# Query and key low parts moved from GpSimd to VectorE, high parts stored by ScalarE, fewer and differently shaped transfers for the score stacks, and longer rings for two loads

## What is computed

```
x = layernorm(x + attn(x))        # 16 heads of 32: softmax(q k^T / sqrt(32)) v,
                                  # blended with a "splat" attention, out projection
x = layernorm(x + ssm(ctx, x))    # u = silu(conv(in_proj ctx)); state = state*exp(delta*A) + delta*u*B_t
                                  # y_t = sum_n state*C_t  over 16 states n, 512 steps; y*silu(x)
x = layernorm(x + ffn(x))         # ternary weights: silu(gate)*up, rms norm, down projection
```

## Time and profile before

| | before |
|---|---|
| median of 3 runs | 1502.52 us |
| the three runs | 1502.21, 1502.52, 1505.94 us |
| profiled execution | 1506.96 us, of which span 1504.9 us |
| mean granted TensorE clock | 0.861 |

### The profile page before, as it was taken

How to read it: one execution, slowest core, us unless ns; L and a number is a source line. 1 busy time by engine, 2 the same in 40 slices (tenths; PEclk the granted TensorE clock), 3 DMA queues, 4 the chain that set the end, 5 groups by cost and what they waited for, 6 DMA issues and landing times.

```text
span 1504.9 us, 14270 instructions
## 1 busy us (share of the span) xinstructions
PE 1215.9 (81%) x4693; PEld 566.1 (38%) x4698; DVE 1208.4 (80%) x1425; ACT 764.5 (51%) x1118; POOL 208.5 (14%) x243
## 2 busy tenths in 40 slices
PE   5563848777779997887989998888899978887996
PEld 4332313332244542332445533333355423333453
DVE  5877988888879998778789996888889996887323
ACT  6765433445367653635466742545476544452231
POOL 1000122001111123100111132100111231001001
PEclk7765877777969998979989998899799989888898
DMA  6853687455328968554239968444169695641131
GB/s 192 275 175 126 145 211 183 98 126 111 85 86 204 256 158 221 140 127 98 52 96 248 232 170 225 99 91 105 51 168 265 163 215 147 143 115 30 63 98 56
DMA packets 113688, 220.18 MB, mean 146 GB/s; under 512 B 15584, under 2 KB 26336, under 8 KB 113616
## 3 DMA queue, kind: packets, MB, share of 16 engines
q1 hardware_dynamic: 94240, 151.25, 33.5%
q0 software_dynamic: 18432, 67.12, 23.1%
q10 hardware_dynamic: 944, 0.92, 0.2%
HBM read 122.37 MB, written 29.62 MB: 101 GB/s over the span
## 4 chain that ended last, share of the span: by engine, by line
PE 35%; DVE 35%; issue 8%; ACT 5%; DMA 5%; POOL 1%; SPq 1%; DVEq 0%; ACTq 0%; POOLq 0%
DVE ST L867 13%; PE ps L1460 8%; DVE ST L859 5%; PE ps L1269 5%; DVE MX L923 5%; PE ps L1252 5%; PE ps L1420 4%; PE ps L1404 3%; DMA WP<-proj_tiles 3%; DVE ST L870 2%; PE ps L1361 2%; PE ps L1333 2%; PE ps L1220 1%; DVE BST L903 1%; ACT dA L568 1%
## 5 line engine op out<-in xcount | busy, mean ns | idle before, releaser
L867 DVE TENSOR_TENSOR_SCAN ST<-dA,ST 128x1024 f32<-128x1024 f32 x128 | 312.5, 2441 | 8.8 <-ACT dA L568 6.0
L1460 PE MATMUL ps<-V,GU 128*128 128x512 f16 x1024 | 239.1, 389 | 5.9 <-DVE V L1054 5.6
L473 POOL DMA_DIRECT2D YA<-ST x128 | 109.7, 857 | 960.2 <-DVE ST L870 911.5
L923 DVE TENSOR_REDUCE MX<-ps 128x1 f32<-128x512 f32 x256 | 165.2, 686 | 90.4 <-PE ps L1252 89.9
L568 ACT ACTIVATE dA<-DL,Aneg 128x511 f32<-128x511 f32 x256 | 168.3, 713 | 79.4 <-DVE ST L867 79.1
L700 ACT ACTIVATE PT<-ps 128x1024 f32<-128x1024 f32 x128 | 126.3, 1020 | 124.8 <-PE ps L1361 124.0
L1252 PE MATMUL ps<-KS,QS 96*128 96x512 f32 x256 | 127.3, 564 | 71.3 <-DVE MX L923 41.6
L870 DVE TENSOR_TENSOR ST<-ST,BC 128x1024 f32<-128x1024 f32 x128 | 159.4, 1246 | 4.4
L859 DVE TENSOR_TENSOR ST<-DU,BC 128x1024 f32<-128x1024 f32 x128 | 155.9, 1218 | 7.1 <-DMA BC<-bc_rows 7.1
L1420 PE MATMUL ps<-WP,QS 128*128 128x512 f32 x512 | 144.6, 426 | 9.3 <-DMA WP<-proj_tiles 8.8
L1460 PEld LDWEIGHTS ps<-V,GU 128*128 128x128 bf16 x1024 | 97.2, 100 | 143.1 <-issue 32.6
(11 more groups left out here) (229 smaller groups left out, 1600.2 us busy)
## 6 DMA issues: line engine op xcount, KB each, us to landing
YA<-ST POOLq DMA_DIRECT2D x128, 512.0 KB, 7.1
BC<-bc_rows SPq DMA_DIRECT2D x64, 512.0 KB, 6.2
qk_parts<-PT SPq DMA_DIRECT2D x64, 256.0 KB, 4.4
GU<-gu_tiles SPq DMA_DIRECT2D x64, 256.0 KB, 7.5
WP<-proj_tiles SPq DMA_DIRECT2D x64, 256.0 KB, 7.1
QS<-qk_parts SPq DMA_DIRECT2D x96, 128.0 KB, 3.4
KS<-qk_parts SPq DMA_DIRECT2D x96, 128.0 KB, 3.8
ST<-in_L_ffn_w_gate_up_dram SPq DMA_DIRECT2D x16, 256.0 KB, 3.3
```

The lines of the kernel that those rows point to most:

```text
L867: nc.vector.tensor_tensor_scan(flat, dA[:, a, :, :].rearrange("p e s -> p (e s)"), flat, 0.0, ALU.mult, ALU.add).then_inc(s_scan, 1)
L923: nc.vector.tensor_reduce(MX[:, j % 2, qt, h:h + 1], ps[:, n % 2, :], AX_X, ALU.max).then_inc(s_mx, 1)
L1460: last = mm(ps[:, f % F_RING, :], GU[:, t % GU_RING, k, m * P:(m + 1) * P], XHL[:, z, k, :], start=(k == 0 and z == 0), stop=(k == KT - 1 ...
```

## The change

1. The low parts leave POOL and are done by DVE, in the order of DVE's program: units 0 to 3 behind the halves at r = 5, 6, 7, 8 (`LOW_BEHIND`), unit 4 behind the half at r = 12, units 5, 6 and 7 behind max tiles 0-3, 4-9 and 10-15.
2. High parts are stored by ACT, right behind the cast, from its own DMA queue; SP keeps the low parts.
3. `qk_parts` in HBM is laid out as (batch, z, head, part, 32, 512) in place of (batch, z, part, 512, 512). A store of one part of a unit is now 4 heads x 32 x 512 with a gap between heads; in exchange the two parts that stand next to each other in a stack come in one load of 64x2x512, so a stack takes 8 loads in place of 12.
4. BC gets three slots in place of two: the load of state n waits for the products of n-3.
5. WP gets four slots and lies in QS[0], whose own tile is free after group 2; its loads stand two tiles further ahead in SP's program.

```diff
-        qk_parts = dram("qk_parts", (B, 2, 2, H, S))
+        qk_parts = dram("qk_parts", (B, 2, NH, 2, D, S))
...
-        BC = sb("BC", [P, 2, 2, S])
+        BC = sb("BC", [P, BC_RING, 2, S])
...
-        WP = sb("WP", [P, 2, H], F32R)
+        WP = QS[0]
...
+        LOW_BEHIND = (5, 6, 7, 8)
...
             def load_bc(bb, n):
-                if type(bb) is not int or bb > 0 or n >= 2:
-                    sp.wait_ge(s_prod, half(bb, n - 2, 1) + 1)
+                if n >= BC_RING:
+                    sp.wait_ge(s_prod, half(bb, n - BC_RING, 1) + 1)
+                else:
+                    since(sp, s_prod, half(bb, 0, 0))
...
-                    first_row = P * j + 2 * D * pair
-                    for r, (zq, zk) in enumerate(((0, 0), (0, 1), (1, 0))):
-                        for z, dst, part in ((0, QS[i], zq), (1, KS[i], zk)):
-                            src = qk_parts[b, z, part, first_row:first_row + 2 * D, :].rearrange("(h p) s -> p h s", p=D)
-                            sp.dma_start(dst[D * r:D * r + D, 2 * pair:2 * pair + 2, :].bitcast(F32), src).then_inc(s_stack[i][pair], 16)
+                    heads = slice(2 * pair, 2 * pair + 2)
+                    for z, dst in ((0, QS[i]), (1, KS[i])):
+                        parts = qk_parts[b, z, HG * j + 2 * pair:HG * j + 2 * pair + 2].rearrange("h a p s -> (a p) h s")
+                        both, high = (slice(D, 3 * D), slice(0, D)) if z == 0 else (slice(0, 2 * D), slice(2 * D, 3 * D))
+                        sp.dma_start(dst[both, heads, :].bitcast(F32), parts).then_inc(s_stack[i][pair], 16)
+                        sp.dma_start(dst[high, heads, :].bitcast(F32), parts[0:D]).then_inc(s_stack[i][pair], 16)
...
                 for u, (j, z) in enumerate(UNITS):
-                    sp.wait_ge(s_hi, 2 * NG * b + u + 1)
-                    sp.dma_start(qk_parts[b, z, 0, P * j:P * j + P, :], QKP[:, u % 2, :].bitcast(F32)).then_inc(s_part[u % 2], 16)
                     sp.wait_ge(s_lo, 2 * NG * b + u + 1)
-                    sp.dma_start(qk_parts[b, z, 1, P * j:P * j + P, :], QKP[:, 2 + u % 2, :].bitcast(F32)).then_inc(s_part[u % 2], 16)
+                    sp.dma_start(qk_parts[b, z, HG * j:HG * j + HG, 1], QKP[:, 2 + u % 2, :].bitcast(F32)).then_inc(s_part[u % 2], 16)
...
+                def load_wp(t):
+                    if t >= WP_RING:
+                        sp.wait_ge(s_dn, NT * b + t - WP_RING + 1)
+                    sp.dma_start(WP[:, t % WP_RING, :].bitcast(F32), proj_tiles[t]).then_inc(s_wp[t % WP_RING], 16)
+
...
                 for t in range(NT):
-                    if t >= 2:
-                        sp.wait_ge(s_dn, NT * b + t - 1)
-                    sp.dma_start(WP[:, t % 2, :].bitcast(F32), proj_tiles[t]).then_inc(s_wp[t % 2], 16)
+                    if t + WP_RING // 2 < NT:
+                        load_wp(t + WP_RING // 2)
...
                     nc.scalar.copy(QKP[:, u % 2, :], bank).then_inc(s_hi, 1)
+                    j, z = UNITS[u]
+                    act.wait_ge(s_hi, 2 * NG * b + u + 1)
+                    act.dma_start(qk_parts[b, z, HG * j:HG * j + HG, 0], QKP[:, u % 2, :].bitcast(F32)).then_inc(s_part[u % 2], 16)
                     for n, a in fill_halves(2 * KT + u, first):
                         exp_dA(b, n, a)
...
-                for r in range(2 * KT):
+                def low_part(u):
+                    dve.wait_ge(s_hi, 2 * NG * b + u + 1)
+                    if u >= 2:
+                        dve.wait_ge(s_part[u % 2], 32 * KT * b + 32 * (u // 2))
+                    nc.vector.tensor_tensor(QKP[:, 2 + u % 2, :], PT[:, 0, u % 2, :], QKP[:, u % 2, :].bitcast(F32),
+                                            ALU.subtract).then_inc(s_lo, 1)
+
+                for r in range(3 * KT):
                     fill_half(r)
-                for u in range(2 * NG):
-                    if u >= NG:
-                        max_tiles(b, 0, X_FIRST[u - NG], X_FIRST[u - NG + 1])
+                    if r in LOW_BEHIND:
+                        low_part(LOW_BEHIND.index(r))
+                for u in range(NG, 2 * NG):
+                    max_tiles(b, 0, X_FIRST[u - NG], X_FIRST[u - NG + 1])
                     fill_half(2 * KT + u)
+                    low_part(u)
```

More of the change, by code:

```diff
@@ L44 @@
 GU_RING = 3
+WP_RING = 4
+BC_RING = 3
 RING = 3
@@ L156, in decoder_layer @@
         s_gu = [sem(f"s_gu{i}") for i in range(GU_RING)]
-        s_wp = [sem(f"s_wp{i}") for i in range(2)]
+        s_wp = [sem(f"s_wp{i}") for i in range(WP_RING)]
         s_gp, s_up, s_sg, s_h, s_hh, s_hl, s_sqa, s_ssq, s_acc, s_dn = (sem(n) for n in (
@@ L164, in decoder_layer @@
             "s_xd", "s_xdc", "s_bcw", "s_dt", "s_abs", "s_rel", "s_spe", "s_ln", "s_dl", "s_du", "s_ya"))
-        s_bc = [sem(f"s_bc{i}") for i in range(2)]
+        s_bc = [sem(f"s_bc{i}") for i in range(BC_RING)]
         s_dA, s_dBu, s_scan, s_prod = (sem(n) for n in ("s_dA", "s_dBu", "s_scan", "s_prod"))
@@ L282, in decoder_layer, with bc_loaded @@
         FILL_BANKS = (0, 2, 1, 0, 2, 1, 0, 1, 6, 7, 0, 1, 6, 7, 6, 7)
-        GU_USES = NT // 2
+        def bc_loaded(bb, n):
+            uses = len(range(n % BC_RING, DS, BC_RING))
+            return 16 * (uses * bb + n // BC_RING + 1)
         def gu_loaded(b, t):
@@ L332, in load_bc @@
                 rows = bc_rows[bb].rearrange("(z n) s -> z n s", z=2)[:, n, :]
-                sp.dma_start(BC[:, n % 2, :, :], rows.partition_broadcast(P)).then_inc(s_bc[n % 2], 16)
+                sp.dma_start(BC[:, n % BC_RING, :, :], rows.partition_broadcast(P)).then_inc(s_bc[n % BC_RING], 16)
             def store_bc(bb):
@@ L395, in load_gu @@
                     sp.dma_start(GU[:, t % GU_RING, :, :].rearrange("p k c -> p (k c)"), gu_tiles[t]).then_inc(s_gu[t % GU_RING], 16)
+                def load_wp(t):
+                    if t >= WP_RING:
+                        sp.wait_ge(s_dn, NT * b + t - WP_RING + 1)
+                    sp.dma_start(WP[:, t % WP_RING, :].bitcast(F32), proj_tiles[t]).then_inc(s_wp[t % WP_RING], 16)
                 for t in range(GU_RING - 1):
                     load_gu(t)
+                sp.wait_ge(s_s, 2 * KT * NG * b + 2 * KT * (NG - 1))
+                for t in range(WP_RING // 2):
+                    load_wp(t)
                 for t in range(NT):
-                    if t >= 2:
-                        sp.wait_ge(s_dn, NT * b + t - 1)
-                    sp.dma_start(WP[:, t % 2, :].bitcast(F32), proj_tiles[t]).then_inc(s_wp[t % 2], 16)
+                    if t + WP_RING // 2 < NT:
+                        load_wp(t + WP_RING // 2)
                     if t + GU_RING - 1 < NT:
@@ L482, in attention_phase @@
                 first = type(b) is int and b == 0
[L483 to L488, removed]
                 for r in range(4 * KT):
-                    if 2 * KT <= r < 3 * KT:
-                        low_part(r - 2 * KT)
                     for n, a in fill_halves(r, first):
                         add_y_behind(b, n, a)
-                    if r >= 3 * KT:
-                        low_part(r - 2 * KT)
                 for z in range(2):
@@ L854, in scan_half @@
                 dve.wait_ge(s_du, bb + 1)
-                dve.wait_ge(s_bc[n % 2], 16 * (DS // 2) * bb + 16 * (n // 2 + 1))
+                dve.wait_ge(s_bc[n % BC_RING], bc_loaded(bb, n))
                 if g >= RING:
@@ L859, in scan_half @@
                 nc.vector.tensor_tensor(ST[:, ring(bb, n, a), :, :], DU[:, 2 * a:2 * a + 2, :],
-                                        BC[:, n % 2, 0:1, :].broadcast_to((P, 2, S)), ALU.mult).then_inc(s_dBu, 1)
+                                        BC[:, n % BC_RING, 0:1, :].broadcast_to((P, 2, S)), ALU.mult).then_inc(s_dBu, 1)
                 if between:
@@ L869, in scan_half @@
                 dve.wait_ge(s_scan, g + 1)
-                nc.vector.tensor_tensor(st, st, BC[:, n % 2, 1:2, :].broadcast_to((P, 2, S)), ALU.mult).then_inc(s_prod, 1)
+                nc.vector.tensor_tensor(st, st, BC[:, n % BC_RING, 1:2, :].broadcast_to((P, 2, S)), ALU.mult).then_inc(s_prod, 1)
             def conv(bb, e):
@@ L1244, in max_scores @@
                     if m % (2 * KT) == 0:
-                        pe.wait_ge(s_stack[i][h // 2], 96 * (2 * b + j // 2 + 1))
+                        pe.wait_ge(s_stack[i][h // 2], 64 * (2 * b + j // 2 + 1))
                     if n >= 2:
@@ L1416, in down @@
                 pe.wait_ge(s_hl, NT * b + t + 1)
-                pe.wait_ge(s_wp[t % 2], 16 * GU_USES * b + 16 * (t // 2 + 1))
+                pe.wait_ge(s_wp[t % WP_RING], 16 * NT // WP_RING * b + 16 * (t // WP_RING + 1))
                 for r in range(KT):
                     for z in range(2):
-                        last = mm(ps[:, 4 + r, :], HL[:, 2 * z + t % 2, r * P:(r + 1) * P], WP[:, t % 2, :],
+                        last = mm(ps[:, 4 + r, :], HL[:, 2 * z + t % 2, r * P:(r + 1) * P], WP[:, t % WP_RING, :],
```

## The result

The changed kernel takes 1608.03 us (median of 4, 1601.07 to 1611.43) against 1503.08 before: ratio 1.0689, 95% interval 1.0648 to 1.073. The profiled execution has a span of 1604.2, 99.3 more than before.

A forecast was written before the change was run, and what follows sets the result against it. PE and DVE, busy 81% and 80%, were taken to bound the kernel in turn by stage. Batch 0 0, stores 3 x 9.0 and rings -4.8 gave +22.2 on the median 1502.52: 1524.7 us, range 1496 to 1552.

The forecast's parts named there:

- The stores' price: Projections, batches 1 to 3: four-engine stores land 4.1 us later each, making tiles 10 to 15 9.0 late a batch.
- rival D: Projection stages: four engines saturate, 88 us of transfers in a stage of 61; 20 a batch, +55, 1558; chance 0.15.
- Where it is lost: Batch 2's projections: delay starts at unit 2's landing and ends at low(6), ahead of tiles 10 to 15, 9.0 us late.
- the delay of an exponential: ScalarE, projections: a high-part store's issue of some 0.6 us between cast and exponential delays one exponential, taken as 0.
- Batch 0: Batch 0's projections: 12.7 us given back against 12.4 for eight low parts; taken as 0, bounds -1 and +5.
- Rings: FFN of batches 0 to 2: longer WP and BC rings remove the waits for WP, -4.8 us in all.
- The BC wait of batch 0: Batch 0's projections: a wait of 7.1 us for BC goes with the longer ring.
- Rival C: Stores on 16 engines and the stalls of low(0) and low(1) vanish: -11.9 us, 1490.6; chance 0.10.
- Low parts on VectorE: Batches 1 to 3: stalls of 1.7 us at low(0) and low(1); 6.9 less 5.6, +1.3 at the first row maximum.
- Rival B: Stores spread over 16 engines, low(6) ahead of tiles 10: -0.9 us, 1501.6, no change; chance 0.20.

The follow-up runs named there:

- e3: The kernel before with the new scratch layout alone (4x32x512 stores, both from SP, eight loads a stack): 1608.34 us, ratio 1.0659.
- e1: The changed kernel with the flat scratch layout, 128x512 stores and twelve stack loads of before: 1505.14 us, ratio 0.9988.
- e2: The changed kernel with its layout and eight loads, each store split into four stores of one head, 32x512: 1521.31 us, ratio 1.0094.
- e5: e1 with the low parts alone stored as 4x32x512, to a tensor with a gap behind each head: 1542.83 us, ratio 1.0254.
- e4: The kernel before with only the BC ring of three and the WP ring of four in QS[0]: 1504.66 us, ratio 0.9973.
- e9: e7 with six stack loads over four heads each in place of twelve: 1529.52 us, ratio 1.016.
- e7: e1 with the low parts of units 0 to 3 on VectorE one half later: 1501.07 us, ratio 0.9951; run again, 1502.22, 0.9977.

## Why the prediction was right and wrong

The direction and the cause were right: the four-step stores ran on four engines, and e3, with e1 and e2 beside it, shows that this alone is the loss. The size was wrong: 1608 lies far above 1524.7 and above the range.

*The stores' price* is the step that failed: "a landing grows by 2.1 (alone) to about 6 (two others in front). I take two, 4.1." In batch 2 it grew by 13.3, 3.2 and 4.6 for units 2, 3 and 4: the first is more than twice the upper bound of 6, the other two are near what was taken. The step priced a store against the stores next to it in an otherwise free engine. But all stores of a stage, the additions to YA, the stack loads and the BC rows go through the same four engines, and I had worked out that these want 88 us in a stage of 61. That was rival D, put at 0.15 and at 20 a batch, with the argument that most of the queue is not waited for. It is: the stores themselves are the queue, and each is waited for by the unit two behind. The shortage worked out there was 27 a batch. From the first high part to the last exponentials batches 1 to 3 lost 26.6, 28.4 and 30.1, and batch 0 lost 17.6. So 4 x 27 - 4.8 = +103, near the measured 105, is helped by luck: batch 0 lost less than 27 and the others somewhat more, and no stage took anything back. The 0.086 us is a mean over all packets of SP's queue, the small end packets among them; ScalarE's packets of 2 KB took 0.090 in e1, which makes the 45 us of a stage's stores 46 and changes nothing. e5 then had the price by the same capacity sum and met it (1545 expected, 1543).

*Where it is lost* was also off. I let the delay begin at unit 2 and end at low(6) ahead of tiles 10 to 15. Low(6) did wait, 6.51, and those tiles came 24.5 late where 9.0 was forecast. But the high part of unit 3, and with it low(3), waited already for unit 1 (6.19, and 4.72 on VectorE), and the exponential behind the high part of unit 4, which waited 8.50, held a scan for 6.35. I had priced nothing of this: the delay of an exponential stood in the sum as 0, though ScalarE's high parts waited for landings before, too. In an in-order stream a late landing holds whatever is queued behind.

*Batch 0* was put at 0 and lost 18.0 between its first and last high part: there too the stores' landings are waited for, and a BC load queued on SP behind the stack came 13.90 late.

*Rings*: -4.8 for the FFN was right: 5.0 in the changed kernel's profile and in e4's, with the waits for WP gone. The BC wait of batch 0 that I counted as gone halved, since the load's place in SP's program did not move.

*Rival C*: its term of -0.8 for batch 0 is worked out nowhere. Without the stalls, eight low parts of 0.7 against 12.7 would give -7.1 there and 1484.3 in place of 1490.6. Nothing measured hangs on it.

*Low parts on VectorE*: the two stalls were forecast as 1.7 and measured as 1.64, and a third, 1.16 at low(2), was not forecast; no scan is lengthened any more. From the start of the halves to the first row maximum, +1.3 was forecast and e1 has 40.75 - 38.6 = +2.1. Rival B's time, 1501.6, a ratio of 0.9994 for stores on sixteen engines, is inside e1's interval.

## What to carry to other kernels

Look at the outermost dimension of both sides of a transfer before a layout is changed for fewer descriptors or issues: here a gap that turned 128 rows into 4 x 32 took the stores from sixteen engines to four. Then price it by capacity, that is all that those engines must carry in the stage against the stage's length, and not by the time of one transfer. Here the sum was 27 over the length, and three of the four batches became 26.6 to 30.1 longer. And count end packets in the queue's total (144 packets a store with sixteen engines, 132 with four here), and how many packets are in flight at once: both told on how many engines the stores ran.

## What the runs showed of the hardware beyond that

- Six stack loads of 256 KB in place of twelve of 128 KB let SP issue the store behind them 5.2 us sooner after the first load, and it landed 1.5 us later, counted from that load (e9, e7).
- Issues on ScalarE's queue took 0.33 us for a flat store (e1), mostly 0.5 to 0.6 for a four-step one, and 1.7 to 4.5 for four stores by heads in one go (e2).
- While PE waited 19.42 for batch 2's first stack, its granted clock fell to 0.50, the 1.2 GHz level, for 966 to 978; over the stage it was 0.77 against 0.89 before. PE's busy time rose from 1215.9 to 1229.0 with the same instructions; that some of the loss is matmuls at the lower clock is likely from this, and not shown. PE's timeline, and the stretch behind it (length, busy times, granted clock, DMA share, GB/s):

```profile
976.58 1.19 PE L1266 MATMUL ps<-KS,QS 96*128 96x512 f32 x2 [19.42 <-DMA KS<-qk_parts]
```

```profile
966.00:978.00 12.00, 1.19 (x2) 0.50 (x2) 4.74 (x5) 2.44 (x5) 0.00 (x0) 0.50 0.63 179
```
